# Decayed attention: order of ScalarE's value scaling, and the step that adds the output product

## The reference, cut to what matters

```python
def step(carry, inp):
    ln, nm, sg = carry
    a_t, b_t, vl_t, vs_t = inp
    ln = _stable_lse(a_t + ln, b_t)
    dec = a_t[..., None] + nm
    new = b_t[..., None] + vl_t[:, None, :]
    m = jnp.maximum(dec, new)
    ssum = sg * jnp.exp(dec - m) + vs_t[:, None, :] * jnp.exp(new - m)
    nsg = jnp.sign(ssum)
    nsg = jnp.where(nsg == 0, jnp.ones_like(nsg), nsg)
    nm = m + jnp.log(jnp.abs(ssum) + EPS)
    y = (nsg * jnp.exp(nm - ln[..., None])).sum(-2)
    return ((ln, nm, nsg), y)
```

## Time and profile before

| | us |
|---|---|
| median of 3 runs (lowest to highest) | 2301.62 (2297.68 to 2303.34) |
| the profiled execution's own time | 2300.68 |
| its span | 2298.8 |
| steps of decayed attention, within the span | about 1714 to 2017 |

### The profile page before, as it was taken

The page is one execution under the profiler, slowest core; times in us unless marked ns, Lnnn a source line. Parts: engine busy times, 40 slices in busy tenths (PEclk is TensorE's granted clock), DMA queues, the critical chain, the costliest instruction groups (busy, mean ns, idle before and its releaser), DMA issues. The chain is left out here.

```text
span 2298.8 us, 29289 instructions
## 1 busy us (share of the span) xinstructions
PE 2048.7 (89%) x9908; PEld 1410.4 (61%) x9908; DVE 1119.8 (49%) x2292; ACT 902.9 (39%) x1668; POOL 122.3 (5%) x137
## 2 busy tenths in 40 slices
PE   7978973899999958999999999999969999867998
PEld 4647762555555547787878777777746666523443
DVE  4655652001101136354453536364448888739992
ACT  5743320111111134444444435354436666525550
POOL 0000003000000011000000000000000000002320
PEclk9989975999999989999999999999988999668999
DMA  7310014787777522010100000012040000010000
GB/s 264 123 51 1 0 65 192 282 315 310 284 314 315 219 69 92 15 46 33 40 32 27 32 27 32 27 46 87 1 162 1 1 1 1 1 78 0 1 14 23
DMA packets 32725, 208.18 MB, mean 91 GB/s; under 512 B 4243, under 2 KB 4244, under 8 KB 25110
## 3 DMA queue, kind: packets, MB, share of 16 engines
q1 hardware_dynamic: 30102, 199.02, 23.0%
q0 software_dynamic: 2560, 8.39, 1.1%
HBM read 186.95 MB, written 20.45 MB: 90 GB/s over the span
## 5 line engine op out<-in xcount | busy, mean ns | idle before, releaser
L108 PE MATMUL PS<-cT,qs 128*128 128x512 f32 x1152 | 295.2, 402 | 9.0 <-ACT pb L1242 7.0
L108 PE MATMUL PS<-pT,cN 128*128 128x512 f32 x1152 | 270.1, 393 | 1.7 <-DVE pT L1337 1.7
L108 PEld LDWEIGHTS PS<-cT,qs 128*128 128x128 f32 x1152 | 209.2, 189 | 59.5 <-issue 15.0
L900 PE MATMUL PS<-W,xgT 128*128 128x384 f32 x736 | 242.8, 489 | 1.4 <-ACT xgT L923 1.4
L108 PEld LDWEIGHTS PS<-pT,cN 128*128 128x128 f32 x1152 | 214.0, 188 | 45.2 <-DVE pT L1337 1.9
L900 PEld LDWEIGHTS PS<-W,xgT 128*128 128x128 f32 x736 | 140.7, 191 | 104.0 <-issue 11.4
L108 PE MATMUL PS<-ws,xT 128*128 128x512 f32 x672 | 183.3, 429 | 6.4 <-DVE ws L571 4.9
L108 PEld LDWEIGHTS PS<-ws,xT 128*128 128x128 f32 x672 | 133.8, 201 | 52.8 <-issue 21.9
L1332 DVE TENSOR_REDUCE nmax<-PS 128x1 f32<-128x512 f32 x128 | 87.7, 685 | 157.0 <-PE PS L108 156.4
L951 DVE TENSOR_TENSOR hid<-gated,PS 128x384 f32<-128x384 f32 x46 | 23.4, 551 | 277.6 <-PE PS L876 235.6
L884 PE MATMUL PS<-W,hT 128*128 128x512 f32 x276 | 124.5, 601 | 10.4 <-ACT hT L917 10.4
(11 more groups left out here) (226 smaller groups left out, 3198.7 us busy)
## 6 DMA issues: line engine op xcount, KB each, us to landing
W<-in_fc SPq DMA_DIRECT2D x23, 3072.0 KB, 12.5
W<-in_proj SPq DMA_DIRECT2D x23, 1536.0 KB, 6.5
cT<-in_ctxT SPq DMA_DIRECT2D x16, 768.0 KB, 5.3
ct_in<-in_ctxT SPq DMA_DIRECT2D x16, 768.0 KB
cn_in<-in_ctxN SPq DMA_DIRECT2D x16, 768.0 KB
W<-in_w SPq DMA_DIRECT2D x2, 4096.0 KB, 12.9
routed_x<-zero SPq DMA_DIRECT2D x23, 256.0 KB, 5.4
xg<-routed_x SPq DMA_DIRECT2D x23, 256.0 KB, 5.7
```

The lines of the kernel that those rows point to most:

```text
L108: mm = nc.tensor.matmul(out, lhs(m, s), rhs(n, s), start=(opens and (s, m, n) == terms[0]), stop=((s, m, n) == terms[-1]))
L900: mm = nc.tensor.matmul(ps[c][:, 0:HFE], xgT[:, k, :], fc[u][:, k, c * HFE:(c + 1) * HFE], start=(k == 0), stop=(k == DK - 1))
```

## The change

ScalarE's `bv` and `ebv` move from the head of step t to the tail of step t - 1, behind `ear` and ahead of the extra piece of that step. Step 0 gets them before the loop. `add_out(c - 1)` moves from step 6 (between s and ep) to step 7 (between ep and sg). No instruction is added or taken away.

```diff
+                def scaled(t):
+                    act.wait_ge(coef, BASE + t // G + 1)
+                    act.wait_ge(vb_mm, BASE + t + 1)
+                    act.wait_ge(s_sb, BASE + 2 * max(t - 1, 0))
+                    nc.scalar.activation(bv[:, t % 2, :], ps[4 + t % VB], ACT.Copy,
+                                         scale=be[:, t:t + 1]).then_inc(bv_sb, 1)
+                    act.wait_ge(ep_sb, BASE + 2 * max(t - 1, 0))
+                    act.sem_inc(seen)
+                    nc.scalar.activation(ebv[:, t % 2, :], ps[4 + t % VB], ACT.Abs,
+                                         scale=ebe[:, t:t + 1]).then_inc(ebv_sb, 1)
+
+                scaled(0)
                 for c in range(NG):
                     for j in range(G):
                         t = G * c + j
-                        act.wait_ge(coef, BASE + c + 1)
-                        act.wait_ge(vb_mm, BASE + t + 1)
-                        act.wait_ge(s_sb, BASE + 2 * max(t - 1, 0))
-                        nc.scalar.activation(bv[:, t % 2, :], ps[4 + t % VB], ACT.Copy,
-                                             scale=be[:, t:t + 1]).then_inc(bv_sb, 1)
-                        act.wait_ge(ep_sb, BASE + 2 * max(t - 1, 0))
-                        act.sem_inc(seen)
-                        nc.scalar.activation(ebv[:, t % 2, :], ps[4 + t % VB], ACT.Abs,
-                                             scale=ebe[:, t:t + 1]).then_inc(ebv_sb, 1)
                         for h, cols in enumerate(HALVES):
                             act.wait_ge(r_sb, BASE + 2 * t + h + 1)
                             act.sem_inc(seen)
                             nc.scalar.activation(ear[:, cols], rb[:, (t - 1) % RB, cols], ACT.Abs,
                                                  scale=eal[:, t:t + 1]).then_inc(ear_sb, 1)
+                        if t + 1 < S:
+                            scaled(t + 1)
                         if j == 0:
                             if c >= 1:
                                 take_y(c - 1)
...
-                        elif j == 6 and c >= 1:
-                            add_out(c - 1)
                         elif j == 7 and c + 1 < NG:
                             weights(c + 1)
                         ve.wait_ge(ebv_sb, BASE + VB + t + 1)
...
+                        elif j == 7 and c >= 1:
+                            add_out(c - 1)
                         for h, cols in enumerate(HALVES):
                             ve.wait_ge(s_sb, BASE + 2 * t + h + 1)
```

## The result

| | us |
|---|---|
| before, median of 4 runs (lowest to highest) | 2302.17 (2297.68 to 2303.34) |
| after, median of 4 runs (lowest to highest) | 2286.40 (2282.48 to 2286.75) |
| ratio, with its 95% interval | 0.9928 (0.9914 to 0.9942) |
| the profiled execution before, after | 2300.68, 2286.63 |

The change is faster by 0.7%, 15.8 us by the medians and 13 to 20 by the interval. The forecast was 2289.0 with a range of 2281 to 2298.

A forecast was written before the change was run, and what follows sets the result against it. The prediction took TensorE's road from head_sums(4) to projection K's end, then VectorE through products, as the bound. 4.85 + 3.4 + 3.5 + 0.9 = 12.6 us gave 2288.1 profiled, 2289.0 as median; range 2281 to 2298.

The forecast's parts named there:

- the waits of 42.1 us: VectorE's waits touched by the change: 22.0 us in seven for the output product, 20.1 us in 13 for bv.
- the two roads to `products`: TensorE's through projection K and VectorE's through take_a, bv, s, ep: both said to arrive by 1844.82, a gain needing both.
- 0.97 us a group: Moved add_out lets head_sums(6) start sooner on TensorE: 0.97 us in each of groups 1 to 5, 4.85 us.
- The clock term: TensorE's half-clock stretches in the groups, left as they were: 0, with 3 us either way.
- The first group: Group c = 0, which has no add_out and whose chain on TensorE is continuous from step 5 on: 0.
- Group 6 and the last: End terms: 3.4 us before head_sums(55) in group 6; 3.5 and 0.9 us around head_sums(63) in the last group.
- The last two terms: Last group: head_sums(63) 3.5 us earlier relative to the product, and 0.9 us shorter close behind it.
- The last product: The last output product shifts rigidly; catching the high clock too was bounded at 0 to 3 us, taken 0.
- the bounds named for the forecast: End terms 0 and +3, group term 0.70 to 1.1, clock 3 us either way: 2284 to 2294, 67%.
- A densely used TensorE: Rival: the denser TensorE keeps its high clock in the groups and the last group, giving 2268 us; chance 4%.
- the third rival: Only part comes: an unseen wait or the clock eats the group gain, or only some terms pay; 2296 us, 20%.
- The slower rival: Half clock reaches further, into projection V, head_sums and values, 3.5 us a group: 2305 us; chance 5%.

The follow-up runs named there:

- the short K: Projection K of groups 1 to 7 made of 4 matmuls, not 12: 2277.42 us on the changed kernel, 2305.43 us on the kernel before.
- the late products: The changed kernel with products moved within step 3 from ahead of ep to behind it: 2275.56 us, ratio 0.9885.

## Why the prediction held

**The bound.** Named rightly: the waits of 42.1 us were not worth 42 us, because TensorE was working through them, and after the change TensorE's road to K is the bound. The predicted wait of about 1 us before `products` is there, 1.16 us seven times, and the short K in the changed kernel showed, at an unchanged clock, that it binds.

**One sentence failed:** that the two roads to `products` were both tight and a gain needed both. The road through take_a begins at projection A on TensorE, so it moved with TensorE (with only `add_out` moved, qk still starts 0.10 us behind K), and `add_out` alone brought everything. ScalarE's part, as the prediction's own later sentence had it, brings nothing alone; it brings nothing beside `add_out` either. What it does is make room of about 1.1 us a group, which the shorter K, the late products and the products of step 4 could each use and which was not there without it.

**0.97 us a group.** The mechanism is as written: 0.97 in the third group, with its 0.94 and 0.81. The sum is not: in the five groups from head_sums(12) to head_sums(52), the profiled executions took 1961.06 - 1776.33 = 184.73 us before and 1957.66 - 1775.39 = 182.27 after, so 2.5 us were won and not 4.85. TensorE's idle time fell by 5.8 us, more than forecast, since 2.2 us of it, waits of 0.56 before head_sums(4), were filled by work at the low clock; its busy time rose by 3.3, as the clock went from 0.92 to 0.89. The clock term, taken as 0 with 3 us either way, so cost 2.4 us here. The first group, for which the forecast has 0, gave 1.3 us (38.30 and 36.97), with its clock at 0.78 before and 0.82 after. Together it is 223.03 less 219.24, 3.8 us from head_sums(4) to head_sums(52). In the kernel with only `add_out` moved the same stretch was 8.5 us shorter than before, with less busy time (202.91 us, clock 0.91):

```profile
1740.18:1954.75 214.57, 202.91 (x854) 0.91 0.00 1
```

**Group 6 and the last.** From head_sums(52) to head_sums(55) it is 1969.26 - 1957.66 = 11.60 us, before 15.45: 3.85, forecast 3.4. From there to the end of the product of group 6 another 1.6 us came, which was not in the sum, because the clock stayed high into this group:

```profile
1971.44 1.03 PE L1542 MATMUL PS<-cn,W 128*128 128x16 f32 x8 [0.26 <-DVE W L1833]
...
1976.95 1.67 PE L1542 MATMUL PS<-cn,W 128*128 128x16 f32 x8 [0.78 <-DVE W L1833]
...
1987.13 5.46 PE L1552 MATMUL PS<-W,yT 128*128 128x512 f32 x8
1992.43 3.02 PE L1542 MATMUL PS<-cn,W 128*128 128x16 f32 x24
1996.62 5.40 PE L1552 MATMUL PS<-W,yT 128*128 128x512 f32 x8 [1.17 <-ACT yT L1634]
```

Before, the low clock came at once with head_sums(55), 1.89 us. The last two terms, 3.5 + 0.9 = 4.4, measured 4.3 (1996.62 less the product's end at 1992.59 is 4.03, before 8.33). The last product took 5.40 us for 6.57: 1.2, inside the bound of 0 to 3 that was taken as 0. Together 3.8 + 3.85 + 1.6 + 4.3 + 1.2 = 14.7 us; the changed kernel's steps began 0.4 us later (head_sums(0) at 1722.57 and 1722.18), which leaves the 14.3 us by which its last addition is earlier (2002.06 and 2016.34), and the 14.2 us between the spans. Against the forecast of 12.6 that is 1.6 + 1.2 us more in the last group and 1.3 in the first, each at a higher clock, 0.45 more in group 6, and 2.4 less in the five groups, at a lower one. That the total came so near is in part luck: these terms of the clock largely cancel, and none was forecast.

Two figures of the working are off without moving the sum. The prediction takes half of 6.57, 3.3 us, for an output product at the full clock; with `products` in step 5 six of them took 3.60, so the low clock cost the one in rows 3 about 2.0 us and not 2.3. And the bounds named for the forecast, all three at their best, give 2282.4 and not 2284.

**The rivals.** A densely used TensorE does not keep its clock by that alone: it was idle 5.0% of the stretch in the changed kernel with the clock at 0.87, and 5.6% with late products with the clock at 0.96. By the rule of the Trainium skill (TensorE: Matmul & The Clock Gate, What's actually happening), activity releases the throttle. The short K in the kernel before goes with it (less work, and 0.86 for 0.89); the short K in the changed kernel does not (less work, 0.87 as before); and the first pair shows that the share of busy time does not tell the clock. Of the third rival a part came: the clock took back 2.4 of the 4.85 us. The slower rival did not come: projection V took 4.62 us in the first group and 3.35 to 3.37 in each of the five others. Why the late products kept the high clock, and whether their place or the length of the group does it, stays open; no experiment here told that apart.

## What to carry to other kernels

A wait on the engine that carries a recurrence is worth only what the other engine of the loop stands idle for it: here a wait of 3.12 us was worth 0.97, most of it TensorE's 0.71 us of idle time before head_sums(6). When two orders are changed together, each alone tells which one pays; the one that pays nothing may still be room that the next change needs (here three times, 9 to 12 us), so it is worth testing again behind each later change. Moving the reader of the binding result behind one more independent instruction (`products` behind ep) brought the next 11 us, 4 of them expected and the rest with the clock. Of the kernels that leave nothing out, three beat the changed one clearly: that one at 2275.6 us, and those with `products` in step 5 at 2274.5 and in step 4 at 2277.3.

## What the runs showed of the hardware

The clock that TensorE is granted moved the time as much as the edits did. The same 852 matmuls took 192.93 to 208.29 us busy over six groups, at granted clocks of 0.96 to 0.87, though the idle time differed by half a microsecond. The effect has either sign: with eight matmuls less in each group the kernel before was slower by 3.4 us (ratio 1.0013, 1.0004 to 1.0023), at 0.86 for 0.89. It also differs between executions of one kernel: with only `add_out` moved, the clock over the whole span was 0.934 in one of 2292.06 us and 0.937 in one of 2283.21.
